# The causal mask of the row-maximum pass: added on VectorE or as a second matrix product

## The reference

```python
def _L0_attn_ref(hidden_states, w_attn, b_attn, w_proj, b_proj):
    qkv = hidden_states @ w_attn.T + b_attn
    q, k, v = ...                                   # (B, H=16, S=512, D=8)
    w = jnp.einsum('bhnd,bhmd->bhnm', q, k) * jax.lax.rsqrt(float(D))
    mask = jnp.tril(jnp.ones((S, S)))
    w = jnp.where(mask > 0, w, -1e9)
    w = jax.nn.softmax(w, axis=-1)
    attn = jnp.einsum('bhnm,bhmd->bhnd', w, v)
    return attn.transpose(0, 2, 1, 3).reshape(B, S, E) @ w_proj.T + b_proj

x = x + _L0_attn_ref(_layernorm(x), ...)            # causal: the stage of this change
x = x + _L0_ffn_ref(_layernorm(x), ...)             # 8 experts, top 2
x = x + _L1_attn_ref(_layernorm(x), ...)            # the same attention without a mask
x = x + _L1_ffn_ref(_layernorm(x), ...)             # FP4-quantised gated network
```

## Time and profile before

| | us |
|---|---|
| median of 3 runs | 2758.33 |
| lowest and highest | 2749.01, 2762.57 |
| profiled execution (the profile gives its span, from the first to the last instruction) | 2764.1 |
| layer 0 attention, in the trace (first L511 to the last of its products) | about 51 to 800 |
| PE busy in the span | 2163.4 (78%) |
| DVE busy in the span | 1812.7 (66%) |

### The profile page before, as it was taken

One profiled execution on the slowest core, in us unless ns is written; L12 is line 12 of the kernel. 1 busy time (PEld: TensorE's weight loads), 2 busy tenths in 40 slices (PEclk: granted clock), 3 DMA queues, 4 the chain that ended last, 5 costly groups with the idle time before them and its releaser, 6 DMA issues. The chain is left out here.

```text
span 2764.1 us, 55527 instructions
## 1 busy us (share of the span) xinstructions
PE 2163.4 (78%) x13643; PEld 1141.0 (41%) x13795; DVE 1812.7 (66%) x5178; ACT 1333.2 (48%) x2917; POOL 901.5 (33%) x1586
## 2 busy tenths in 40 slices
PE   3898999999964346999559988888888899746665
PEld 1454544555533335989413322322222233224444
DVE  4777877788835342222178877778777788379995
ACT  0465666666640012444206655656565667723332
POOL 4433333333116661000343433333333331044441
PEclk9899999999975557999759998999999999968887
DMA  5222122212101114444222211112121221000000
GB/s 154 76 66 84 60 82 63 87 56 90 52 18 41 34 37 116 134 133 133 73 86 68 59 59 55 54 55 66 55 66 56 67 64 48 1 4 12 15 12 20
DMA packets 154223, 173.57 MB, mean 63 GB/s; under 512 B 38440, under 2 KB 122096, under 8 KB 153840
## 3 DMA queue, kind: packets, MB, share of 16 engines
q1 hardware_dynamic: 144320, 153.33, 18.4%
q0 software_dynamic: 8192, 16.79, 2.1%
q10 hardware_dynamic: 1456, 0.60, 0.1%
HBM read 119.78 MB, written 49.28 MB: 61 GB/s over the span
## 5 line engine op out<-in xcount | busy, mean ns | idle before, releaser
L614 ACT ACTIVATE l_probs<-bank 128x512 f32<-128x512 f32 (+3 forms) x2048 | 971.7, 519 | 604.5 <-PE bank L527 234.9
L511 PE MATMUL bank<-k_stack,q_stack 96*128 96x512 bf16 (+3 forms) x2048 | 723.3, 359 | 97.1 <-DMA k_stack<-scratch 48.3
L710 DVE TENSOR_REDUCE l_rowmax<-bank 128x1 f32<-128x512 f32 x1024 | 641.8, 682 | 201.2 <-PE bank L511 125.2
L524 PE MATMUL bank<-q_stack,k_stack 128*128 128x512 bf16 x1897 | 643.6, 346 | 77.5 <-ACT l_probs L614 70.6
L707 DVE CUSTOM_DVE_ANT_0 bank<-bank,mask_rows_q 128x512 f32<-128x512 f32 (+3 forms) x1024 | 481.1, 516 | 160.1 <-PE bank L511 126.6
L540 PE MATMUL bank<-l_probs,v_aug 128*32 128x512 f32 (+3 forms) x4096 | 474.2, 535 | 19.8 <-ACT l_oT L648 15.9
L524 PEld LDWEIGHTS bank<-q_stack,k_stack 128*128 128x128 bf16 x2048 | 200.2, 98 | 567.8 <-ACT l_probs L614 415.2
L465 POOL CAST l_rowmax_parts<-l_rowmax 128x16 bf16<-128x16 f32 x128 | 25.3, 198 | 995.3 <-DVE l_rowmax L710 548.2
L511 PEld LDWEIGHTS bank<-k_stack,q_stack 96*128 96x128 bf16 x2048 | 203.0, 99 | 304.1 <-DVE l_rowmax L710 99.4
L527 PE MATMUL bank<-mask_rows_k,ident_bf 128*128 128x128 bf16 x1024 | 218.6, 220 | 26.0 <-DMA q_stack<-l_rowmaxT 17.1
L1470 ACT ACTIVATE experts_hT<-bank,experts_b 128x256 f32<-128x256 f32 x288 | 120.8, 471 | 166.4 <-PE bank L1442 164.9
(11 more groups left out here) (229 smaller groups left out, 2600.4 us busy)
## 6 DMA issues: line engine op xcount, KB each, us to landing
q_stack<-scratch SPq DMA_DIRECT2D x384, 96.0 KB
k_stack<-scratch SPq DMA_DIRECT2D x384, 96.0 KB
experts_w<-in_w SPq DMA_DIRECT2D x72, 256.0 KB, 2.5
scratch<-l_q_parts SPq DMA_DIRECT2D x32, 384.0 KB, 2.6
scratch<-l_k_parts SPq DMA_DIRECT2D x32, 384.0 KB, 3.3
experts_rows<-rows_in SPq DMA_DIRECT2D x72, 128.0 KB, 2.1
rows_out<-experts_y SPq DMA_DIRECT2D x72, 128.0 KB, 2.2
q_stack<-l_rowmaxT SPq DMA_DIRECT2D x384, 4.0 KB, 2.2
```

The lines of the kernel that those rows point to most:

```text
L511: nc.tensor.matmul(bank[:, 0:keys(t)], q_stack[n % 2][0:MAXROW, h, t * P:(t + 1) * P], k_stack[n % 2][0:MAXROW, h, 0:keys(t)], start=True, ...
L524: last = nc.tensor.matmul(bank[:, first(t):S], k_stack[n % 2][:, h, t * P:(t + 1) * P], q_stack[n % 2][:, h, first(t):S], start=True, stop ...
L614: nc.scalar.activation(probs[:, u % PSLOTS, c0:S], st_bank[bank_of(u)[0]][:, c0:S], ACT.Exp, scale=SCALE).then_inc(exp_done, 1)
L710: nc.vector.tensor_reduce(rowmax[:, g % 2, c:c + 1], scores, X_AXIS, ALU.max).then_inc(max_done, 1)
```

## The change

In the first pass of layer 0, the mask is no longer added by VectorE. After the product of a unit, TensorE adds a second product into the last 128 columns of the same bank: `ident_bf` as the stationary and the own tile of `mask_rows_q` as the moving operand, 128 columns in bf16. `s_mm` is raised by this second product. VectorE then takes the plain maximum with the instruction of layer 1, writes nothing back, and the empty instruction of `held` ahead of it is gone.

```diff
@@ scores_for_max (TensorE)
                 t = TT - 1 - t
-                nc.tensor.matmul(bank[:, 0:keys(t)], q_stack[n % 2][0:MAXROW, h, t * P:(t + 1) * P],
-                                 k_stack[n % 2][0:MAXROW, h, 0:keys(t)], start=True, stop=True).then_inc(s_mm, 1)
+                last = nc.tensor.matmul(bank[:, 0:keys(t)], q_stack[n % 2][0:MAXROW, h, t * P:(t + 1) * P],
+                                        k_stack[n % 2][0:MAXROW, h, 0:keys(t)], start=True, stop=not causal)
+                if causal:
+                    last = nc.tensor.matmul(bank[:, keys(t) - P:keys(t)], ident_bf[:, :], m["mask_rows_q"][:, S - P:S],
+                                            start=False, stop=True)
+                last.then_inc(s_mm, 1)
@@ take_max (VectorE)
-                if causal:
-
-                    held(dve, b)
-                    nc.vector.tensor_tensor_reduce(scores, scores, m["mask_rows_q"][:, S - keys(t):S], 1.0, LOWEST,
-                                                   ALU.add, ALU.max, rowmax[:, g % 2, c:c + 1]).then_inc(max_done, 1)
-                else:
-                    nc.vector.tensor_reduce(rowmax[:, g % 2, c:c + 1], scores, X_AXIS, ALU.max).then_inc(max_done, 1)
+                nc.vector.tensor_reduce(rowmax[:, g % 2, c:c + 1], scores, X_AXIS, ALU.max).then_inc(max_done, 1)
```

## The result

The change made the kernel slower: 2789.91 us (median of 4 runs, 2780.62 to 2797.25) against 2759.03 (4 runs), a ratio of 1.0106 with a 95% interval of 1.0073 to 1.0139, so +29 us, or +31 by the medians. Forecast were +35.8 us and 2794. The profiled execution has a span of 2777.2 us.

A forecast was written before the change was run, and what follows sets the result against it. TensorE was taken to bound layer 0's bodies with both passes. Terms 53.8 - 9 - 5 - 2 - 2 = +35.8 us on the profiled 2764.1, less 5.8 to match the median, gave 2794 us, range 2778 to 2816.

The forecast's parts named there:

- TensorE sets the pace: Layer 0's bodies with both passes: TensorE streams without a pause, VectorE has 125 of 600 us to spare; chance 0.72.
- 51 that were reckoned for it: Rival, VectorE as the pace in the first pass: 1024 units save 0.05 us each, giving 2707 us; chance 0.06.
- 0.056 us a product: Added mask products in bodies 0 to 14: 960 at 0.056 us each, +53.8 us, all on the path.
- 81 ns: Skill page's figure per weight load and matmul pair at 128 columns: an estimated 78 us for the added products, 2818 in all.
- 0.099 of the weight load: Rival: each added product's weight load is not hidden and costs 0.099 us, so +77 and 2835 us; chance 0.10.
- What the pauses take back: TensorE's waits in layer 0 and batch 0's first pass were to offset the added products by 9, 5, 2 and 2 us.
- Quad 14, -9 us: Each body's quad 14: TensorE's wait for a bank behind VectorE's 1.25 us of statistics goes, 0.6 us a body, -9 us.
- Operands, -5 us: Start of bodies with a new batch: TensorE arrives later, so its waits for operands go, -5 us.
- ScalarE's copy, -2 us: Before the v-products: added products fill 0.1 to 0.2 of each 0.25 us wait for ScalarE's copy, -2 us.
- Batch 0's first pass, -2 us: Body -1, VectorE partly the pace: 64 units gain at most 3.2 us, operands' DMA takes some back, -2 us.
- The plain maximum: VectorE, first pass: 0.05 us less a unit than the masked maximum, 51 us of VectorE over 1024 units.
- Two bodies grow by 5 to 7 us: Sign of being right: the distance between two turns of the loop, two bodies, grows by 5 to 7 us.

The follow-up runs named there:

- VectorE's part alone: Changed kernel without the added product: plain maximum, no mask in the first pass; ratio 0.9989 to the kernel before.
- the repetition: The changed kernel run again as it stands, beside runs of the kernel before; ratio 1.0123, layer 0 at 810 us.
- the run with the statistics spread: Kernel before with layer 0's layernorm statistics spread over quads 6, 9, 10, 13 and 14 instead of all at 14; ratio 1.0020.
- first pair: The first measurement of the change: 2789.91 us against 2759.03 for the kernel before, ratio 1.0106; chip not on record.

## Why the prediction was right, and which terms were off

*TensorE sets the pace:* right. The product alone gives +35 us; VectorE's part alone gives 3 us of the 51 that were reckoned for it. The bodies without a turn of the loop and without a half-clock stretch show it best. From one batch's output projection to the next they took, from the third body on, 43.1 us before (42.9 to 43.5), no less without the mask (42.8 to 43.7), 45.9 in the change and 49.0 with the product twice. The first product adds 64 x 0.056 = 3.6 us to a body and takes 0.8 us of PE's idle time (1.5 to 0.7), which leaves the 2.8 measured.

*0.056 us a product:* right in the rows (0.055 to 0.06 in the stream) and shown to follow the columns (0.03 at 64). The 81 ns that the Trainium skill's "TensorE: Matmul & The Clock Gate" gives in "Back-to-back issue gap" did not appear, and neither did the 0.099 of the weight load.

*What the pauses take back:* about right in sum, 54 - 18 = 36 forecast. PE's idle time fell by 17 us in 600, or 19 in the 670 us of the bodies with both passes, and 54 - 19 = 35 is what the product alone measured. (In the repetition it fell by 13 us, to 26.6, so this balance holds to some 5 us.) The prediction had given half of it to VectorE's speed.

*Quad 14, -9 us:* the mis-sized step. I wrote that VectorE gains over "the dozen units for which VectorE runs without a pause"; it is four, as VectorE last waits for PE just before them. The wait goes because PE is later: from 6.0 us to 2.1 with the product alone, and only to 4.5 with the plain maximum alone. When it went without a later PE, in the run with the statistics spread, the operands' DMA became late in its place. What VectorE gives is 2 to 3 us in this kernel. As PE's own growth closes the wait anyway, the total hardly noticed; that a term with half of its mechanism wrong left the sum right is luck.

*The clock* is no term of the sum. Of the 600 us it was half for 23.9 before and 23.9 after, so leaving it out cost nothing here. In the experiments it was half for 0 to 47.8 us, and by an estimate, half of the difference to 23.9, that is worth up to 12 us of time either way. Effects of a few microseconds between two experiments are not safe from it.

*Operands, -5 us, and ScalarE's copy, -2 us:* the rows fell from 4.6 to 2.2 us and from 3.8 to nothing, together about what was taken. *Batch 0's first pass, -2 us:* at most half of it came. From the first L511 to that of body 0 it took 37.7 us where it had taken 38.9 (38.7 in the repetition). That product waits 4.75 us for its operands where it waited 2.42, so the DMA took back most of the gain, as the prediction had allowed. *The plain maximum:* the starts of 384, 256 and 128 columns, which no row of before had, stand 0.465, 0.33 and 0.20 apart against 0.515, 0.38 and 0.26; so 0.05 held at all widths in a stream without a pause. For the first unit behind a wait, which the prediction did not set apart, it is only 0.01 at 256 to 512 columns (0.616 to 0.608 at 512). It fits that VectorE's busy time fell by 40 us and not by 51.

*Two bodies grow by 5 to 7 us:* 5.9.

## What to carry to other kernels

Before work is moved from one engine to another, read from the distances of starts which of the two streams without a pause; the one that does pays in full, less only the pauses that it has left, and the relieved one gives little. A wait that looks like the price of a slow engine may only be the first of several that are late at nearly the same time: remove it alone and see who is next. Compare the granted clock of two profiles as well before a few microseconds are put down to an engine. And a wait that recurs at a fixed distance in the program, with a releaser that has long been done, is worth a run of its own, whatever the change at hand is about.

## What the runs showed of the hardware

- A turn of the loop that runs on all engines left PE without a product for 3.0 to 4.8 us in layer 0, and behind it stood products at 1.2 GHz for 3 to 7 us, once 10. Writing ten bodies out in both attentions gave 2.5%; the longer code cost nothing that the runs show.
- Waits for operands can have half-clock products behind them too. In the kernel without mask and loop five such waits of 1.8 to 3.0 us, each with products at 1.2 GHz behind it, add up to 31 us at half the clock in 600. Without the loop on the kernel before, four of 1.5 to 1.9 us had them behind one alone (3.4 us), and with the added product and no loop, where the only one over 1 us was 1.2 us long, the clock was full throughout.
- The plain maximum from PSUM is faster than the masked one with its read-out by 0.05 us at every width from 128 to 512 columns in a stream without a pause, and by 0.01 us behind a wait at 256 to 512.
- A matmul of 64 bf16 columns, with a weight load of 128 columns of its own, held the next one up by 0.03 us.
- The same kernel took 2670 us on one chip and 2753 on another, and 2759 in the first pair. In the profiles the routing stage differed most for its length, 181.5 against 218 to 222 us; layer 1's attention, with the loop, took 979 to 984 us on the chip of 2670 us and 1044 and 1027 in the first pair.
